# TensorE waits for a maximum product's PSUM bank ahead of the score product of the same pack, instead of between the two

## What is computed

```python
x = L0_attn_x                                     # (8, 512, 256)
xn = _layernorm(x)
x = x + _L0_attn_ref(xn, ...) * _silu(_L0_ffn_ref(xn, ...))
xn = _layernorm(x)
x = x + _L1_attn_ref(xn, ...) * _silu(_L1_ffn_ref(xn, ...))

# layer 0: 16 query heads in 4 groups, distance bias, causal
scores = einsum('bqgrd,bkgd->bgrqk', q, k) * scale + bias
attn = softmax(scores); o = einsum('bgrqk,bkgd->bqgrd', attn, v); return o @ Wo.T
# layer 1: 32 half heads, causal softmax of each, differences of pairs
attn = softmax(einsum('bhtd,bhsd->bhts', q, k) + causal)
attn = attn[:, :, 0] - lam * attn[:, :, 1]; out = einsum('bhts,bhsd->bhtd', attn, v)
```

## Time and profile before

| | |
|---|---|
| three runs | 2347.73, 2348.24, 2362.52 us (median 2348.24) |
| the profiled execution's own time | 2355.72 us, of which the span of its instructions is 2353.8 us |
| PE busy | 2117.3 us, 90% of the span |
| PEld busy | 1437.2 us, 61% |
| DVE busy | 1372.4 us, 58% |
| ACT busy | 893.6 us, 38% |
| POOL busy | 683.5 us, 29% |
| DMA | 240.51 MB, 102 GB/s on average |

### The profile page before, as it was taken

The page is one execution under the profiler, slowest core; times in us unless marked ns, Lnnn a source line. Parts: engine busy times, 40 slices in busy tenths (PEclk is TensorE's granted clock), DMA queues, the critical chain, the costliest instruction groups (busy, mean ns, idle before and its releaser), DMA issues.

```text
span 2353.8 us, 33709 instructions
## 1 busy us (share of the span) xinstructions
PE 2117.3 (90%) x12290; PEld 1437.2 (61%) x12386; DVE 1372.4 (58%) x2691; ACT 893.6 (38%) x1749; POOL 683.5 (29%) x845
## 2 busy tenths in 40 slices
PE   2299998999989999999989999999998999989898
PEld 1157556575666656676565755757556675656656
DVE  4465655656556565556647566475565666655664
ACT  2142451425424253333524345152451425433352
POOL 2332331313313233223323233141331323322331
PEclk7589999999999999999999999999999999999999
DMA  6823423243222533116231252323422253321530
GB/s 207 287 63 101 144 68 95 72 143 100 84 70 64 166 100 104 37 55 197 85 88 54 85 166 70 102 65 121 122 78 76 72 155 102 98 51 55 173 98 14
DMA packets 105604, 240.51 MB, mean 102 GB/s; under 512 B 17048, under 2 KB 27288, under 8 KB 105184
## 3 DMA queue, kind: packets, MB, share of 16 engines
q1 hardware_dynamic: 91184, 194.41, 27.4%
q0 software_dynamic: 14256, 43.94, 6.4%
HBM read 179.67 MB, written 57.82 MB: 101 GB/s over the span
## 4 chain that ended last, share of the span: by engine, by line
PE 63%; DMA 11%; DVE 7%; SPq 4%; ACT 4%; issue 3%; POOL 2%; DVEq 0%; ACTq 0%; POOLq 0%
PE bank L387 17%; PE bank L467 11%; PE bank L546 10%; PE bank L483 9%; PE bank L436 8%; DMA upring<-up_img 3%; DMA qring<-mneg 3%; DMA k_img<-probs 3%; PE bank L440 3%; PE bank L565 2%; ACT probs L624 2%; DMA kring<-k_img 2%; SPq L334 2%; SPq L351 2%; DVE nmax L718 2%
## 5 line engine op out<-in xcount | busy, mean ns | idle before, releaser
L718 DVE TENSOR_REDUCE nmax<-bank 128x1 f32<-128x512 f32 (+3 forms) x1056 | 651.3, 639 | 366.2 <-PE bank L440 353.7
L387 PE MATMUL bank<-xnT,upring 128*128 128x512 f32 (+1 forms) x2208 | 623.8, 405 | 24.6 <-DMA upring<-up_img 23.7
L624 ACT ACTIVATE probs<-bank 128x512 f32<-128x512 f32 (+1 forms) x864 | 469.1, 560 | 345.9 <-PE bank L467 331.8
L467 PE MATMUL bank<-qring,kring 128*128 128x512 f32 (+1 forms) x1056 | 478.2, 456 | 54.6 <-ACT probs L624 24.6
L436 PE MATMUL bank<-kring,qring 127*128 127x512 f32 (+3 forms) x1536 | 461.5, 353 | 50.9 <-DMA kring<-k_img 47.4
L387 PEld LDWEIGHTS bank<-xnT,upring 128*128 128x128 f32 x2208 | 396.4, 192 | 106.2 <-issue 33.5
L436 PEld LDWEIGHTS bank<-kring,qring 127*128 127x128 f32 x1536 | 272.9, 195 | 127.3 <-DMA kring<-k_img 50.3
L546 PE MATMUL bank<-wdown,hbuf 128*128 128x256 f32 x1408 | 338.9, 391 | 0.0
L467 PEld LDWEIGHTS bank<-qring,kring 128*128 128x128 f32 x1056 | 206.3, 197 | 189.2 <-ACT probs L624 100.1
L1494 POOL TENSOR_SCALAR_AFFINE_SELECT probs<-probs 128x512 f32<-128x512 f32 x256 | 163.2, 638 | 511.5 <-ACT probs L624 509.4
L546 PEld LDWEIGHTS bank<-wdown,hbuf 128*128 128x128 f32 x1408 | 267.6, 196 | 34.9 <-issue 1.7
(11 more groups left out here) (119 smaller groups left out, 1532.3 us busy)
## 6 DMA issues: line engine op xcount, KB each, us to landing
upring<-up_img SPq DMA_DIRECT2D x176, 512.0 KB, 3.9
q_img<-probs SPq DMA_DIRECT2D x96, 256.0 KB, 4.2
qring<-q_img SPq DMA_DIRECT2D x256, 64.0 KB, 1.9
kring<-k_img SPq DMA_DIRECT2D x64, 256.0 KB, 3.1
qring<-q_img SPq DMA_DIRECT2D x32, 384.0 KB, 4.9
k_img<-probs SPq DMA_DIRECT2D x48, 256.0 KB, 4.6
up_img<-hbuf POOLq DMA_DIRECT2D x22, 512.0 KB, 4.9
gring<-gate_img POOLq DMA_DIRECT2D x32, 256.0 KB, 3.7
```

Of the source, the lines that this page charges most:

```text
L387: last = nc.tensor.matmul(out_ap, part_a(a, pa, k), part_b(b, pb, k), start=(n == 0), stop=(n == len(steps) - 1))
L467: nc.tensor.matmul(SC[n % 2][:, 0:heads * w].rearrange("p (g n) -> p g n", g=heads), kring[l][:, ks, kt * P:(kt + 1) * P], qring[l][:, s, ...
L624: nc.scalar.activation(pr, pr if biased else scores, ACT.Exp, scale=scale).then_inc(s_exp, 1)
L718: nc.vector.tensor_reduce(nmax[:, u % 2, g0:g0 + heads, qt], MX[n % 2][:, 0:heads * w].rearrange("p (g n) -> p g n", g=heads), AX.X, ALU.m ...
```

## The change

`pe_max_pack` loses its wait, which becomes a function of its own, `pe_max_bank`. In `unit`, that function is called ahead of the score pack; in the other places where max packs are issued it is called directly ahead of `pe_max_pack`, where the wait stood already. No matmul, reduce, copy or DMA is added, removed or moved.

```diff
+        def pe_max_bank(pe, u, i):
+
+            k, done = mx(u)
+            n = PACKS * done + i
+            if n >= 2:
+                pe.wait_ge(s_mr[k], so_far(s_mr[k], n - 1))
+
         def pe_max_pack(pe, u, i):
             ...
-            if n >= 2:
-                pe.wait_ge(s_mr[k], so_far(s_mr[k], n - 1))
             bk = MX[n % 2]
...
                     if more:
                         wait_ring(pe, u + 1)
                     for i in range(PACKS):
+                        if more:
+                            pe_max_bank(pe, u + 1, i)
                         pe_score_pack(pe, u, i)
                         if more:
                             pe_max_pack(pe, u + 1, i)
```

More of the change, by code:

```diff
@@ L954, in _ @@
                 for i in range(PACKS):
+                    pe_max_bank(pe, 0, i)
                     pe_max_pack(pe, 0, i)
@@ L1210, in pe_batch @@
                 for i in range(PACKS):
+                    pe_max_bank(pe, UNITS[0], i)
                     pe_max_pack(pe, UNITS[0], i)
```

## The result

The changed kernel takes 2407.76 us (median of 4 runs, 2406.58 to 2409.35), the kernel before 2352.48 (4 runs, 2347.73 to 2362.52). The ratio is 1.0239, 95% interval 1.0213 to 1.0264: 55 us slower, where 57.5 us was forecast. The profiled executions differ by 51.8 us in their spans (2405.6 and 2353.8).

The account below looks back on a forecast made before the run. TensorE's order of work was taken to bound layer 1's units; 52.1 (layer 1) + 2.4 (layer 0) + 3 (row) = 57.5 us on the 2348.24 median gave 2406 us. Range 2375 to 2440, with 0.80 chance.

Parts of the forecast that it names:

- What bounds it: In layer 1's units TensorE's order of work sets the pace; standing still adds 0.93 us a unit, 52.1 over 56.
- The ring: Loop through the two maximum banks, score i to score i + 2: 1.59 us with the score inside, TensorE needs 1.20.
- Score 10 and the transpose: End of a layer 1 unit: score 10 at 3.07 and transpose of maxima at 5.03 us after score 6, 0.59 later.
- Layer 0: 24 units: free in units 1 and 2 except late reduces, partly absorbed; 0.1 us each, 2.4, between 0 and 8.
- the second wait: The wait as its own instruction ahead of a score: taken as nothing; 0.05 at some four stalls a unit, 11 us.
- The row: The row of maxima's DMA, behind five ring loads that come 0.15 us closer to it: 3 us, between 0 and 8.
- The sum: Layer 1, layer 0 and row terms, 52.1 + 2.4 + 3 = 57.5 us, giving 2406 us by the median.
- Not slower: Rival: VectorE's reduces stay back to back with later scores, so nothing is lost, 2348 us; chance 0.08 for within 1%.
- Every pack pays for the extra instruction: Rival: 863 more instructions on TensorE cost 0.05 us each, 43 us on top, 2449 us; chance 0.06.
- The clock falls: Rival: new stalls in the 56 layer 1 units lower TensorE's granted clock, up to 158 us, 2564 us; chance 0.04.

## Why the prediction held

**What bounds it.** Right. TensorE's order of work set the unit's pace, and the loss arrived in the unit's length: layer 1's stretches from first score to transpose grew by 46.9 us over 56 units, 0.84 each. The forecast term was 52.1, 0.93 each. This is the one large term, and it was about 10% too big.

**The ring.** Right where it could be read: 1.59 us for two packs at score 2 (1.57 between the matmuls), 1.34 at score 8. The experiments agree: +52 us for layer 1 alone, at most 9 for layer 0, and a cost that fell from 55 to 31 us as the reduce was shortened. A ring of three banks, the plainest test, was not tried, since all eight PSUM banks are in use.

**Score 10 and the transpose.** Mis-sized, 2.99 and 4.91 after score 6 instead of 3.07 and 5.03. I took 0.99 us from score 8 to its reduce as now (1417.03 to 1418.02 in the earlier trace rows). It was 1160.40 - 1159.50 = 0.90. The 0.99 held a stall that the change removes: in the kernel before, the max product of pack 8 waits there for the reduce of pack 6, its weight load starting 0.32 behind the score's (1417.35), where it is 0.11 in the changed kernel (1159.61). From score 10 to the transpose it is 1.92 and not 1.96. There the working had the wrong end: it added the length of the product with v (0.84), where the reduce of pack 10 releases the transpose, in the kernel before too (1419.69 to 1420.38, transpose at 1420.44). The product path would end 0.08 us sooner (0.77 from product to transpose with halved reduces, 0.85 here), so it cost little. The 0.08 and 0.04 too much, less 0.03 too little for packs 0 to 5 (0.37 measured, 0.34 worked out), make up the 0.09 of the unit's term.

**Layer 0.** The size was right, the cause was not. 2.4 us were forecast, from late reduces that are only partly absorbed; the stretches of units 0 to 2 grew by 2.4 us. In unit 0 the delay arrives at score 10 (13.22 instead of 12.77 after score 0) and is nearly all taken up before the transpose (15.14 against 15.10); the sum over the batches is 1.3 us longer, but among the kernels that leave layer 0 as it was this sum already runs from 1.0 below to 1.3 above, so it isn't shown to be the move. In units 1 and 2 (1.1 us) the ring did bind, unlike the working: score 2 comes 0.07 later, as the scores in front stand 1.53 and not 1.64 for two packs, and score 5 comes 0.49 later where up to 0.34 was worked out. Pack 6's wait for the exp absorbed all of that, and the 0.07 us a unit that is left is the second wait at pack 6. I had set the second wait at nothing, because the bank of the maximum would end last. That is true where layer 1 is held, and not for this pack. That 2.4 was both forecast and measured is partly luck.

**The row.** 3 us were forecast; the waits in the two traces differ by 18.0 - 12.3 = 5.7. The mechanism shows in the time of issue (0.72 to 0.95 us behind the transpose, where 0.15 more was worked out). Its size isn't settled, as the waits alone scatter by about 6 us between executions: with the wait moved in layer 0 only they are 18.2.

**The sum.** 46.9 + 2.4 + 5.7 = 55.0, and the spans differ by 51.8; the stretches between the layers and at the ends of batches, which differ by some us from one execution to another, hold the other -3.2. The forecast of 2406 against 2407.76 is closer than its terms: the rise was set 2 us too high, and the kernel before was taken at 2348.24, where four runs give 2352.48. That the two nearly cancel is luck.

**The rivals.** *Not slower* fell with the hole in VectorE's reduces. *Every pack pays for the extra instruction* fell with the second wait that was met long before: 5 us, not 43. *The clock falls* didn't happen here: 0.962 beside 0.963, and no low stretch in units 5 to 10. But it does in this kernel where units start behind stalls of 2.4 us.

## What to carry to other kernels

A wait placed in an in-order queue makes everything behind it part of the loop it guards. Before moving one, add up the loop from release to release with the new members in it and compare it with what each engine needs for the same work: here 1.59 against 1.20 for two packs, so 0.4 us for each pair that isn't covered by other work. Put a wait directly ahead of its first real user, and keep useful work between two waits. And look at the held weight loads, not only at the matmuls' own waits, to see how near to its edge such a loop already is.

## What was not expected of the hardware

- A matmul of this program carries one wait; a second one is an instruction of its own. It delays the matmul by 0.06 us where it is the last to be met (0.05 us from the exp's end to the load it releases with one wait, 0.11 with two). Met early, 847 more of them went with +5 us in all, between 1 and 10.
- The kernel before waits for its reduces in the matmul records for 2.7 us, and yet halving them gained 38 us. A held weight load shows up here as a longer or later matmul rather than as idle time: 0.75 us from score to score instead of 0.60.
- The row's DMA is slowed by the ring loads issued ahead of it and not by the engine that issues it: medians of 3.40 us from the transpose to its landing from ScalarE, 3.42 from SP, 2.41 with the loads behind it.
- The granted clock was at its low level for 326 us instead of 175 with stalls of 1.9 to 3.6 us between units of layer 1, in 41 of the 48 units behind them, and in none of these units with the changed kernel's stalls of 0.14 to 0.5 us a pack. Single waits for the row did it too: in the traces with the loads in their old place, a low stretch followed 10 of the 13 waits of 1.7 to 2.4 us and none of the 7 of 1.5 to 1.6.
